# Values of four heads over a batch as a two by two block product in seven multiplications, from the third group of heads on

## The chip, the cores and the metric

The kernel runs on one core of a Trainium2 chip. The time is device microseconds of one execution, lower is better; three runs stand behind the time before. "Shares" and "busy" are of the profiled execution's span, from its first to its last instruction.

## The reference

A transformer block over x of 2 batches x 512 tokens x 512 features, all in float32. The part that the change touches is the attention's value projection:

```python
x1 = _layernorm(x)                       # 2 x 512 x 512
q, k, v = x1 @ Wq + bq, x1 @ Wk + bk, x1 @ Wv + bv    # each 512 -> 4096, 32 heads of 128
q, k = rms_norm(q, gq), rms_norm(k, gk)
attn = softmax(q k^T / sqrt(128))        # for each batch and head, 512 x 512
out = (attn @ v) @ Wo + bo               # 4096 -> 512
x = x + _layernorm(out)
```

Behind it comes a feed-forward part (a dense layer and eight gated experts of rank 16), layernorm and sum again. It isn't touched.

## The kernel before, in words

Every float32 product is made of float16 halves: an operand is scaled by a power of two and split into a high half (float16 of it) and a low half (what is left), and a product is three matmuls, high x high, high x low, low x high, added up in PSUM (`three`, lines 1234 to 1238). ScalarE makes most high halves, VectorE or GpSimd the low ones. So three matmuls stand for one, and TensorE's columns are what there is most of.

The work runs in stages. Up to some 340 us: layernorm of x, its transposed halves `xh` and `xl`, and then q and k of all 32 heads (`phase_a` on each engine), stored to DRAM; beside it GpSimd adds up squares for the norms. From there to some 1010 us: attention. Then the feed-forward part.

Attention goes by pairs of heads (`PAIRS` = 16), with the loop over two pairs at a time; `par` is 0 for an even pair, 1 for an odd one. A pair has four steps `s`, for (batch 0, head 0), (batch 0, head 1), (batch 1, head 0), (batch 1, head 1); n = 4p + s. There is no planner: each engine runs a hand-written order of its own, the function `step`, and semaphores join them. There are eight PSUM banks: four for scores, two (`YB`) for the rows of the output projection, one (`VB`) for values, one (`OB`) for the attention's output. Of a step:

- **TensorE** (`step`, line 1424): `scores` of step n, 12 matmuls of 512 columns into four banks, each bank after its low half of step n-1 is made (`low_ready`); `values`, one item of 24 matmuls of 256 columns (two tiles of 128 tokens x 256 value columns), for a pair that comes later; `rows`, 12 matmuls of the output projection, after the sums that read those banks are made (`y_added`); `attend` of step n-1, 12 matmuls.
- **VectorE** (`step`, line 2071): `maxima` of the four score banks; `add_rows`, which adds the two products of the previous step's `rows` into `y`; `inverses` (reciprocal, and `row_inv`, a scaling of five columns); `low_halves`, four; `split_v`, the low half of a value item; `scores_down` for the next step.
- **ScalarE** (`step`, line 1047): reads the output of `attend` (`o_t`); four exponentials; the high half of the next keys (`high_k`); four high halves of the probabilities, after `row_inv`; `evacuate_v`, the high half of a value item; the high half of a piece of weights.
- **GpSimd** (`step`, line 763): halves of the output (`split_o`), `scale_k`, low halves of weights (`split_wo` in steps 0 and 3, `split_wv` in steps 1 and 2: a scaling and a subtraction each), `low_k`.
- **SP's queue** (`step`, line 545): loads of q and k, of weights, and the transposes of the probabilities' halves (`pair_q` to `pair_k`).

The wait in `rows`, and the addition on VectorE that answers it:

```python
1415                        pe.wait_ge(y_added, 2 * n - 7 + k)
...
2069                    add_y(2 * n - 5 + k, 2 * ((s + 1) % 4) + k, YB + k, to).then_inc(y_added, 1)
```

The second is in `add_rows`, which step n of VectorE calls with n - 1, so both speak of the same sum.

## Time and profile before

| | before |
|---|---|
| median of 3 runs | 1071.59 us (1071.46 to 1071.72) |
| span of the profiled execution | 1069.7 us |
| median less that span (what lies around it) | 1.9 us |
| TensorE busy | 1052.9 us, 98% |
| VectorE busy | 789.6 us, 74% |
| ScalarE busy | 741.3 us, 69% |
| GpSimd busy | 681.1 us, 64% |
| granted TensorE clock, mean | 0.998 of full |
| a step of attention in the loop | 10.39 us |

The page gives the span of the profiled execution and not its whole time; the median of the runs stands for that. In the tables PE is TensorE, PEld its weight loads, DVE VectorE, ACT ScalarE, POOL GpSimd, SP SyncE. "busy" of a group is the sum of its instructions, "idle before" the time in which their engine stood still just ahead of them, with what ended it. In a timeline, "x4" is four like instructions in a row; their starts can be closer than their durations, since an operation's end overlaps the next one's start. A matmul of 512 columns shows 0.38 us, though the next begins 0.215 us later.

### The profile page before, as it was taken

What the parts mean: (1) busy time and instruction counts of PE and PEld (TensorE: products, weight loads), DVE (VectorE), ACT (ScalarE), POOL (GpSimd) and SP (SyncE); (2) the same over time, 40 slices, a digit from 0 to 9 for tenths busy, and PEclk for the clock granted to TensorE, in tenths of its full rate; (3) what the DMA queues carried; (4) which work ended last, traced back from release to release, by engine and by line L of the source; (5) the groups of instructions that cost most, each with busy time, mean ns of one, the idle gap of its engine ahead of it and who ended that gap; (6) DMA issues with size and microseconds to landing.
All of it is one profiled execution on the core that took longest, in us unless ns stands there. A gap on an engine that the chain in (4) does not pass through costs nothing.

```text
span 1069.7 us, 20038 instructions
## 1 busy us (share of the span) xinstructions
PE 1052.9 (98%) x5781; PEld 563.7 (53%) x5781; DVE 789.6 (74%) x1831; ACT 741.3 (69%) x1470; POOL 681.1 (64%) x597
## 2 busy tenths in 40 slices
PE   7999999999999999999999999999999999999997
PEld 4444444444445655555555555555555555555454
DVE  8767766666645887777777777777777777778887
ACT  4666766666656787676777767677776767777756
POOL 2667767676657476676666667666666766666713
PEclk9999999999999999999999999999999999999999
DMA  6688985656663679977676776767677676765702
GB/s 240 175 237 261 269 232 194 223 215 222 203 142 135 199 187 267 227 173 177 177 184 165 189 179 165 176 178 187 162 190 179 163 176 180 189 163 128 175 33 79
DMA packets 312072, 197.76 MB, mean 185 GB/s; under 512 B 275424, under 2 KB 279392, under 8 KB 312032
## 3 DMA queue, kind: packets, MB, share of 16 engines
q1 hardware_dynamic: 304400, 193.71, 65.5%
q10 hardware_dynamic: 7632, 3.57, 1.5%
q8 instruction: 18, 0.29, 0.1%
q14 instruction: 22, 0.18, 0.1%
HBM read 94.45 MB, written 35.68 MB: 122 GB/s over the span
## 4 chain that ended last, share of the span: by engine, by line
PE 91%; DVE 5%; ACT 2%; DMA 1%; issue 1%; SPq 0%; POOL 0%; DVEq 0%; ACTq 0%
PE ps L1236 30%; PE ps L1237 30%; PE ps L1238 30%; DMA wa_stage<-w_qk 1%; DVE pair_q L2061 1%; ACT ps L1031 0%; DVE ps L2047 0%; DVE stats L1630 0%; DMA pair_k<-pair_q 0%; ACT xh L1024 0%; ACT pair_q L1040 0%; PE ps L1348 0%; DVE y L2011 0%; DVE wa_lo L1735 0%; DVE y L2172 0%
## 5 line engine op out<-in xcount | busy, mean ns | idle before, releaser
L2047 DVE TENSOR_SCALAR_CACHE_REDUCE ps<-ps,score_down 128x512 f32<-128x512 f32 x256 | 177.5, 756 | 88.6 <-PE ps L1238 87.9
L2061 DVE SCALAR_TENSOR_TENSOR pair_q<-ps,row_inv,pair_q 128x512 f16<-128x512 f32 x256 | 174.5, 744 | 54.7 <-ACT pair_q L1040 54.6
L1031 ACT ACTIVATE ps<-ps,neg_max 128x512 f32<-128x512 f32 x256 | 168.2, 657 | 44.9 <-DVE ps L2047 44.9
L1236 PE MATMUL ps<-xh,wa_hi 128*128 128x512 f16 x512 | 194.3, 379 | 1.8 <-DVE wa_lo L1735 1.8
L1237 PE MATMUL ps<-xl,wa_hi 128*128 128x512 f16 x512 | 194.3, 379 | 0.0
L1238 PE MATMUL ps<-xh,wa_lo 128*128 128x512 f16 x512 | 194.3, 379 | 0.0
L1040 ACT ACTIVATE pair_q<-ps,row_inv 128x512 f16<-128x512 f32 x256 | 154.9, 688 | 21.5 <-DVE row_inv L2054 21.5
L758 POOL CAST oth<-o_t 128x512 f16<-128x512 f32 x62 | 37.8, 609 | 201.0 <-ACT o_t L1005 200.9
L664 POOL TENSOR_TENSOR acc<-acc,squares 128x512 f32<-128x512 f32 x120 | 151.1, 1281 | 1.7 <-ACT squares L882 1.7
L1237 PE MATMUL ps<-wv_lo,xh 128*128 128x256 f16 x512 | 139.7, 273 | 0.0
L1236 PE MATMUL ps<-wv_hi,xh 128*128 128x256 f16 x512 | 139.7, 273 | 0.0
L1238 PE MATMUL ps<-wv_hi,xl 128*128 128x256 f16 x512 | 139.7, 273 | 0.0
L655 POOL TENSOR_TENSOR qk_out<-q_s,qk_out 128x512 f16<-128x512 f32 x64 | 74.8, 1170 | 95.3 <-ACT qk_out L891 95.3
L882 ACT ACTIVATE squares<-ps,q_k_bias,qk_down 128x512 f32<-128x512 f32 x128 | 99.0, 785 | 43.0 <-PE ps L1238 28.8
L1005 ACT ACTIVATE o_t<-ps,tab 128x512 f32<-128x512 f32 x62 | 42.6, 688 | 108.0 <-PE ps L1238 108.0
L1840 DVE TENSOR_SCALAR qk_out<-ps,k_b,k_g 128x512 f32<-128x512 f32 x64 | 51.8, 809 | 84.9 <-ACT squares L882 84.9
L1236 PE MATMUL ps<-wo_hi,oth 128*128 128x512 f16 x256 | 97.2, 380 | 1.3 <-DVE otl L2038 0.6
L1236 PE MATMUL ps<-k_hi,qk_in 128*128 128x512 f16 x256 | 97.2, 380 | 0.3 <-DVE qk_out L1840 0.3
L1238 PE MATMUL ps<-k_hi,qk_in 128*128 128x512 f16 x256 | 97.2, 380 | 0.0
L1237 PE MATMUL ps<-k_lo,qk_in 128*128 128x512 f16 x256 | 97.2, 380 | 0.0
L1238 PE MATMUL ps<-wo_hi,otl 128*128 128x512 f16 x256 | 97.2, 380 | 0.0
L1237 PE MATMUL ps<-wo_lo,oth 128*128 128x512 f16 x256 | 97.1, 379 | 0.0
(236 smaller groups left out, 2220.9 us busy)
## 6 DMA issues: line engine op xcount, KB each, us to landing
q_k_scratch<-qk_out SPq DMA_DIRECT2D x64, 512.0 KB, 3.9
qk_in<-q_k_scratch SPq DMA_DIRECT2D x64, 512.0 KB, 3.4
wa_stage<-w_qk SPq DMA_DIRECT2D x32, 512.0 KB, 4.8
u_stage<-w_vo SPq DMA_DIRECT2D x32, 512.0 KB, 5.5
wv_stage<-w_vo SPq DMA_DIRECT2D x16, 512.0 KB, 4.2
wo_stage<-w_vo SPq DMA_DIRECT2D x16, 512.0 KB, 4.4
qk_tops<-qk_top_scratch ACTq DMA_DIRECT2D x27, 128.0 KB, 4.2
y<-x SPq DMA_DIRECT2D x8, 256.0 KB, 5.4
```

Source lines behind the costliest of these rows:

```text
L655: pool.tensor_tensor(pair(qk_out[:, par, b, 1, :])[:, 1, :], q_s[:, par, b * S:(b + 1) * S], pair(qk_out[:, par, b, 1, :])[:, 0, :], ALU.s ...
L664: pool.tensor_tensor(acc[:, w, cols], acc[:, w, cols], squares[:, par, w, cols], ALU.add).then_inc(acc_ready, 1)
L882: act.activation(squares[:, par, w, b * S:(b + 1) * S], ps[:, 4 * par + g, :], ACT.Square, bias=q_k_bias[:, par, w:w + 1], scale=qk_down[: ...
L1005: act.activation(o_t[:, s % 2, :], ps[:, OB, :], ACT.Identity, bias=tab[:, 4, bass.ds(h, 1)], scale=O_DOWN).then_inc(o_t_ready, 1)
L1031: act.activation(ps[:, SCORE + i, :], ps[:, SCORE + i, :], ACT.Exp, bias=neg_max[:, sl, i:i + 1], scale=-1.0, accum_out=row_sum[:, sl, i:i ...
L1040: act.activation(pair_q[:, 0, i, :], ps[:, SCORE + i, :], ACT.Identity, scale=row_inv[:, sl, i:i + 1]).then_inc(high_ready, 1)
L1236: pe.matmul(outp, lhs[0], rhs[0], start=first, stop=False)
L1237: pe.matmul(outp, lhs[0], rhs[1], start=False, stop=False)
L1238: return pe.matmul(outp, lhs[1], rhs[0], start=False, stop=last)
L1840: dve.tensor_scalar(qk_out[:, par, b, 0, :], ps[:, 4 * par + 2 * b + 1, :], k_b[:, slot:slot + 1], k_g[:, slot:slot + 1], ALU.add, ALU.mul ...
L2047: dve.tensor_scalar(ps[:, SCORE + i, :], ps[:, SCORE + i, :], score_down[:, sl, i:i + 1], None, ALU.mult, ALU.min, accum_out=neg_max[:, sl ...
L2061: dve.scalar_tensor_tensor(out=pair_q[:, 1, i, :], in0=ps[:, SCORE + i, :], scalar=row_inv[:, sl, i:i + 1], in1=pair_q[:, 0, i, :], op0=AL ...
```

## The change

The value projection of one batch is a product of 512 tokens x 512 features with 512 features x 512 columns, for four heads (two pairs). It is cut into blocks of 256: A11, A12, A21, A22 of x and B11 to B22 of the weights. Plain, that is eight block products. The new form uses seven products of sums of blocks and adds the results up (the scheme known as Winograd's form of Strassen's). It is used for 24 of the 32 heads: the first 8 heads (two groups of four) keep the old form. What changes, engine by engine:

- **Ahead of the loop**: GpSimd makes the four sums of x, each in halves, for both batches (`sums_of_x`, 32 operations, spread over eight rounds of its stage of the projections, whose loop is unrolled for it).
- **Weights**: a group's two pairs are loaded into two buffers. GpSimd makes four differences of blocks (`first_term`, `second_terms`, `fourth_term`); ScalarE seven high halves, VectorE seven low halves (`low_block`), which GpSimd made before (`split_wv`, four per group, goes).
- **Products** (`products`): a "window" of four steps (one pair) makes the values of one batch of a group: two products of 12 matmuls of 256 columns in steps 0, 1 and 3, one in step 2, in the banks `OB` and `VB`. The window of batch 0 is run in the odd pair before the group, that of batch 1 in the group's own even pair. Windows fill pairs 3 to 14.
- **Results**: ScalarE reads two of a window's products to SBUF (`v_first`, `v_fourth`), VectorE adds five up (`plus`), GpSimd two (`join`, in the next pair); ScalarE makes four high halves, GpSimd four low ones (`low_alpha` in steps 2 and 3, `low_beta` in step 1 of the next pair).
- **Items of the old form** are taken forward: steps 1.0 to 1.2 (pair 1, steps 0 to 2) make one, steps 1.3 to 2.2 two each, step 2.3 none. Steps 0 to 3 of pair 15 make no values.
- Some powers of two for the scaling change, `vh` and `vl` are twice as wide, and semaphores are shared, to no effect on the order.

The core of the diff. Lists of steps and of waits are shortened at "...":

```diff
+            def first_term(quad):
+                pool.wait_ge(wv_loaded, 16 * (quad + 2))
...
+                pool.wait_ge(second_loaded, 16 * quad)
+                pool.tensor_tensor(wt_1[:, :, :], wv_second[:, 0:2, :], wv_stage[:, 0:2, :],
+                                   ALU.subtract).then_inc(v_terms, 1)
...
+            def second_terms(quad):
+                q = quad - W_FROM
+                pool.wait_ge(v_terms, 4 * q + 1)
...
+                pool.wait_ge(wt_lo_ready, 7 * q + 1)
+                pool.tensor_tensor(wv_stage[:, 0:2, :], wv_second[:, 2:4, :], wt_1[:, :, :],
+                                   ALU.subtract).then_inc(v_terms, 1)
+                pool.tensor_tensor(wv_second[:, 0:2, :], wv_second[:, 2:4, :], wv_second[:, 0:2, :],
+                                   ALU.subtract).then_inc(v_terms, 1)
+            def fourth_term(quad):
+                pool.wait_ge(v_terms, 4 * (quad - W_FROM) + 3)
+                pool.tensor_tensor(wt_4[:, :, :], wv_stage[:, 2:4, :], wv_stage[:, 0:2, :],
+                                   ALU.subtract).then_inc(v_terms, 1)
+            def join(w):
+                pool.wait_ge(v_saved, 2 * w + 2)
...
+                pool.wait_ge(v_added, 5 * w + 5)
+                pool.tensor_tensor(v_joint, v_third[:, :, :], v_fourth[:, :, :], ALU.add).then_inc(v_joined, 1)
+                pool.tensor_tensor(v_fourth[:, :, :], v_second[:, :, :], v_fourth[:, :, :],
+                                   ALU.add).then_inc(v_joined, 1)
+            def low_beta(w, b):
+                for i, src in ((1, v_joint), (0, v_fourth[:, :, :])):
+                    pool.wait_ge(beta_high, 2 * w + 2 - i)
+                    pool.tensor_tensor(v_tiles(vl, b, i, 1), src, v_tiles(vh, b, i, 1),
+                                       ALU.subtract).then_inc(beta_ready, 1)
+            def low_alpha(w, b, i):
+                pool.wait_ge(alpha_high, 2 * w + 2 - i)
+                pool.tensor_tensor(v_tiles(vl, b, i, 0), v_sum[:, :, :], v_tiles(vh, b, i, 0),
+                                   ALU.subtract).then_inc(alpha_ready, 1)
...
+            def step(p, s, par, prepare=True, weights=True, left=None, terms=None, first=False, half=None, window=None):
                 n = 4 * p + s
                 split_o((s - 2) % 4, n - 2)
                 if prepare:
                     scale_k(p + s // 2, (s + 2) % 4)
+                if left is not None and s == 0:
+                    join(left[0])
+                if left is not None and s == 1:
+                    low_beta(*left)
+                if window is not None and s >= 2:
+                    low_alpha(*window, 3 - s)
                 if weights:
                     if s == 0:
-                        split_wo(p, par, 1, n - 2)
-                    if s == 1:
-                        split_wv(p + 1, 1 - par, 0, n - 2)
+                        split_wo(p, par, 1)
+                    if s == 3:
+                        split_wo(p + 1, 1 - par, 0)
+                if terms is not None:
+                    if s == (2 if first else 1):
+                        first_term(terms)
                     if s == 2:
-                        split_wv(p + 1, 1 - par, 2, n - 2)
+                        second_terms(terms)
                     if s == 3:
-                        split_wo(p + 1, 1 - par, 0, n - 2)
+                        fourth_term(terms)
+                if half is not None:
...
+            def values_early(w, b, s):
+                if s == 0:
+                    act.wait_ge(v_part, 7 * w + 1)
+                    act.activation(v_first[:, :, :], bank_of_values(OB), ACT.Copy, scale=V_DOWN).then_inc(v_saved, 1)
+                if s >= 2:
+                    act.wait_ge(v_added, 5 * w + 1 + s)
+                    act.activation(v_tiles(vh, b, 3 - s, 0), v_sum[:, :, :], ACT.Copy).then_inc(alpha_high, 1)
+            def values_late(w, b, s):
+                if s == 3:
+                    act.wait_ge(v_part, 7 * w + 7)
...
+                        act.wait_ge(beta_ready, 2 * w)
+                    act.activation(v_fourth[:, :, :], bank_of_values(VB), ACT.Copy, scale=V_DOWN).then_inc(v_saved, 1)
...
+            def product(left, block, b, bank):
+                for t in range(2):
+                    for k, half in enumerate(left(b, t)):
+                        ins = three(ps[:, bank, t * WIDE:(t + 1) * WIDE], half,
+                                    (wt_hi[:, block, k], wt_lo[:, block, k]), k == 0, k == 1)
+                ins.then_inc(v_part, 1)
...
+                if s != 2:
+                    pe.wait_ge(o_t_ready, n - 1)
+                if s == 0:
+                    block_ready(1)
...
+                    product(a(0, 0), B11, b, OB)
+                    block_ready(2)
...
+                        pe.wait_ge(v_saved, 2 * w)
+                    product(x_sum_of(1), T2, b, VB)
+                if s == 1:
+                    block_ready(3)
+                    product(x_sum_of(2), T3, b, OB)
+                    block_ready(4)
+                    pe.wait_ge(v_added, 5 * w + 1)
+                    product(a(1, 1), T4, b, VB)
+                if s == 2:
+                    block_ready(5)
+                    pe.wait_ge(v_added, 5 * w + 3)
+                    product(a(0, 1), B21, b, VB)
+                if s == 3:
+                    block_ready(6)
+                    product(x_sum_of(3), B22, b, OB)
+                    block_ready(7)
+                    pe.wait_ge(v_added, 5 * w + 4)
+                    product(x_sum_of(0), T1, b, VB)
...
+            def step(p, s, par, items=(), window=None, quad=None):
                 n = 4 * p + s
                 pe.wait_ge(qk_lo_ready, n + 1)
                 scores(n, s)
-                values(p, s, par, n)
+                if items:
+                    values(items[0])
+                if window is not None:
+                    products(*window[0:2], s, window[2], n)
                 rows(p, s, par, n)
-                attend(n - 1, (s - 1) % 2, (s - 1) % 4 // 2)
+                if len(items) > 1:
+                    values(items[1])
+                if window is not None:
+                    outputs_bank_read(window[0], s)
+                values_ready(s, par, quad)
...
+            def plus(to, bank, saved):
+                dve.scalar_tensor_tensor(out=to[:, :, :], in0=ps[:, bank, :].rearrange("p (t n) -> p t n", t=2),
+                                         scalar=V_DOWN, in1=saved[:, :, :], op0=ALU.mult,
+                                         op1=ALU.add).then_inc(v_added, 1)
...
+            def values_early(w, b, s):
+                if s == 1:
+                    dve.wait_ge(v_part, 7 * w + 3)
+                    plus(v_third, OB, v_second)
+                if s == 3:
+                    dve.wait_ge(v_part, 7 * w + 6)
+                    plus(v_second, OB, v_second)
+            def values_late(w, b, s):
+                if s == 0:
+                    dve.wait_ge(v_part, 7 * w + 2)
...
+                    dve.wait_ge(v_saved, 2 * w + 1)
...
+                        dve.wait_ge(v_joined, 2 * w)
+                    plus(v_second, VB, v_first)
+                if s == 1:
+                    dve.wait_ge(v_part, 7 * w + 4)
...
+                        dve.wait_ge(alpha_ready, 2 * w)
...
+                    dve.wait_ge(v_added, 5 * w + 2)
+                    plus(v_sum, VB, v_third)
+                if s == 2:
+                    dve.wait_ge(v_part, 7 * w + 5)
...
+                    dve.wait_ge(alpha_ready, 2 * w + 1)
+                    plus(v_sum, VB, v_first)
+            def low_block(quad, count, block, src):
+                dve.wait_ge(wt_hi_ready, 7 * (quad - W_FROM) + count)
+                dve.scalar_tensor_tensor(out=wt_lo[:, block], in0=src, scalar=v_up[:, :], in1=wt_hi[:, block],
+                                         op0=ALU.mult, op1=ALU.subtract).then_inc(wt_lo_ready, 1)
+            def low_early(quad, s, par):
+                if (s, par) == (2, 0):
+                    low_block(quad, 1, B11, wv_stage[:, 0:2, :])
+                if (s, par) == (0, 1):
+                    low_block(quad, 3, T3, wv_second[:, 0:2, :])
+                if (s, par) == (2, 1):
+                    low_block(quad, 6, B22, wv_second[:, 2:4, :])
+            def low_late(quad, s, par):
+                if (s, par) == (3, 0):
+                    low_block(quad, 2, T2, wv_stage[:, 0:2, :])
+                if (s, par) == (0, 1):
+                    low_block(quad, 4, T4, wt_4[:, :, :])
+                if (s, par) == (1, 1):
+                    low_block(quad, 5, B21, wv_stage[:, 2:4, :])
+                if (s, par) == (2, 1):
+                    low_block(quad, 7, T1, wt_1[:, :, :])
...
+            def step(p, s, par, items=(), rows=True, down=True, to=None, window=None, quad=None):
                 n = 4 * p + s
                 sl = s % 2
                 maxima(n, sl)
                 if rows:
                     add_rows((s - 1) % 4, n - 1, to)
+                if window is not None:
+                    values_early(*window, s)
+                if quad is not None:
+                    low_early(quad, s, par)
                 inverses(n, sl)
+                if len(items) > 1:
+                    split_v(items[0], VB)
                 for i in range(TB):
                     low_halves(n, sl, i)
-                if value:
-                    split_v(n + 2, 2 * ((s + 1) % 4), VB)
+                if items:
+                    split_v(items[-1], VB)
+                if window is not None:
+                    values_late(*window, s)
+                if quad is not None:
+                    low_late(quad, s, par)
...
+            step(1, 0, 1, items=(6,))
+            step(1, 1, 1, items=(7,))
+            step(1, 2, 1, items=(8,))
+            step(1, 3, 1, items=(9, 10))
+            step(2, 0, 0, items=(11, 12))
+            step(2, 1, 0, items=(13, 14))
+            step(2, 2, 0, items=(15, 16))
+            step(2, 3, 0)
             for s in range(4):
-                step(1, s, 1)
-            with pe.Fori(1, PAIRS // 2 - 1) as i:
+                step(3, s, 1, window=(0, 0, 0))
+            with pe.Fori(W_FROM, QUADS - 1) as i:
                 for s in range(4):
-                    step(2 * i, s, 0)
+                    step(2 * i, s, 0, window=(2 * i - 3, 1, i - 2), quad=i)
                 for s in range(4):
-                    step(2 * i + 1, s, 1)
+                    step(2 * i + 1, s, 1, window=(2 * i - 2, 0, i - 1), quad=i)
             for s in range(4):
-                step(PAIRS - 2, s, 0)
-            step(PAIRS - 1, 0, 1)
-            step(PAIRS - 1, 1, 1)
+                step(PAIRS - 2, s, 0, window=(2 * QUADS - 5, 1, QUADS - 3), quad=QUADS - 1)
+            step(PAIRS - 1, 0, 1, quad=QUADS - 1)
+            step(PAIRS - 1, 1, 1, quad=QUADS - 1)
```

## Rows read from the trace of the kernel before

**Rows 1.** The page: TensorE busy over the span, and the chain by engine.

```profile
PE 1052.9 (98%) x5781; PEld 563.7 (53%) x5781; DVE 789.6 (74%) x1831; ACT 741.3 (69%) x1470; POOL 681.1 (64%) x597
...
PE 91%; DVE 5%; ACT 2%; DMA 1%; issue 1%; SPq 0%; POOL 0%; DVEq 0%; ACTq 0%
```

**Rows 2.** Busy time by engine in one stretch of the loop, clock, DMA.

```profile
682.00:764.00 82.00, 82.00 (x476) 46.45 (x475) 62.59 (x144) 60.04 (x128) 54.43 (x48) 1.00 0.67 175
```

**Rows 3.** Timeline of one loop step: start us, duration us, engine, line, names.

```profile
702.34 0.38 PE L1236 MATMUL ps<-k_hi,qk_in 128*128 128x512 f16 x1
...
702.71 0.69 ACT L1005 ACTIVATE o_t<-ps,tab 128x512 f32<-128x512 f32 x1 [1.89 <-PE ps L1238]
...
703.19 0.76 DVE L2047 TENSOR_SCALAR_CACHE_REDUCE ps<-ps,score_down 128x512 f32<-128x512 f32 x1 [1.60 <-PE ps L1238]
...
704.93 0.27 PE L1236 MATMUL ps<-wv_hi,xh 128*128 128x256 f16 x1
...
705.37 1.28 POOL L721 TENSOR_TENSOR qk_in<-qk_in,rms_row 128x512 f32<-128x512 f32 x1
...
705.88 1.41 DVE L2005 SCALAR_TENSOR_TENSOR y<-ps,y_down,y 128x512 f32<-128x512 f32 x2
...
706.62 1.57 POOL L687 TENSOR_SCALAR wv_stage<-wv_stage,v_up 128x512 f32<-128x512 f32 x1
...
706.73 0.62 ACT L988 ACTIVATE k_hi<-qk_in 128x512 f16<-128x512 f32 x1
...
707.41 0.17 DVE L2054 TENSOR_SCALAR row_inv<-row_rec 128x5 f32<-128x5 f32 x1
...
707.55 0.38 PE L1236 MATMUL ps<-wo_hi,oth 128*128 128x512 f16 x1
...
708.52 2.73 DVE L2061 SCALAR_TENSOR_TENSOR pair_q<-ps,row_inv,pair_q 128x512 f16<-128x512 f32 x4 [0.93 <-ACT pair_q L1040]
...
711.16 0.68 DVE L1997 SCALAR_TENSOR_TENSOR vl<-ps,vh 128x512 f16<-128x512 f32 x1
...
711.75 0.22 DVE L1947 TENSOR_SCALAR score_down<-rms,exp_scale 128x5 f32<-128x5 f32 x1
...
712.73 0.38 PE L1236 MATMUL ps<-k_hi,qk_in 128*128 128x512 f16 x1
...
713.58 0.76 DVE L2047 TENSOR_SCALAR_CACHE_REDUCE ps<-ps,score_down 128x512 f32<-128x512 f32 x1 [1.60 <-PE ps L1238]
```

**Rows 4.** Timeline of the last step: two waits for a VectorE result.

```profile
1003.79 0.76 DVE L2047 TENSOR_SCALAR_CACHE_REDUCE ps<-ps,score_down 128x512 f32<-128x512 f32 x1 [0.18 <-DVE score_down L1947]
...
1008.61 2.73 DVE L2061 SCALAR_TENSOR_TENSOR pair_q<-ps,row_inv,pair_q 128x512 f16<-128x512 f32 x4
...
1009.42 0.39 PE L1236 MATMUL ps<-wo_hi,oth 128*128 128x512 f16 x1 [0.43 <-DVE pair_q L2061]
```

**Rows 5.** Groups by line and form, 560 to 1000 us: busy us, mean ns.

```profile
L2061 DVE SCALAR_TENSOR_TENSOR pair_q<-ps,row_inv,pair_q 128x512 f16<-128x512 f32 x168 | 114.5, 744 | 38.0 <-ACT pair_q L1040 38.0
...
L2005 DVE SCALAR_TENSOR_TENSOR y<-ps,y_down,y 128x512 f32<-128x512 f32 x86 | 60.5, 745 | 0.0
L721 POOL TENSOR_TENSOR qk_in<-qk_in,rms_row 128x512 f32<-128x512 f32 x42 | 53.3, 1269 | 0.0
L727 POOL TENSOR_TENSOR k_lo<-qk_in,k_hi 128x512 f16<-128x512 f32 x42 | 48.6, 1157 | 0.9 <-ACT k_hi L988 0.9
```

**Rows 6.** Timeline at 998 us: one GpSimd, one small VectorE operation.

```profile
998.11 1.16 POOL L689 TENSOR_TENSOR wb_lo<-x_first,wb_hi 128x512 f16<-128x512 f32 x1
...
998.34 0.96 DVE L2054 TENSOR_SCALAR row_inv<-row_rec 128x5 f32<-128x5 f32 x1
```

**Rows 7.** Timeline of GpSimd at 316 us, two additions of the projection stage.

```profile
316.40 2.95 POOL L664 TENSOR_TENSOR acc<-acc,squares 128x512 f32<-128x512 f32 x2
```

**Rows 8.** Timeline of VectorE at 317 us, two low halves of weights.

```profile
317.39 2.51 DVE L1735 SCALAR_TENSOR_TENSOR wa_lo<-wa_stage,qk_up,wa_hi 128x512 f16<-128x512 f32 x2
```

**Rows 9.** Waits between 60 and 380 us: total us, times, longest.

```profile
POOL qk_out L655 <- ACT qk_out L891: 84.3, 27, 10.2
```

568 lines of the change are left out of this document (397 added, 171 removed).

## The prediction, before the change was run

> **What bounds the kernel now.** I read the page first: TensorE is busy for 98% of the span and is 91% of the chain that ended last [rows 1]. A stretch of eight steps shows the same in the attention loop, at the full granted clock: 82 of 82 us on TensorE, with VectorE at 62.6, ScalarE at 60.0 and GpSimd at 54.4 [rows 2]. So columns taken off TensorE can shorten the loop, as long as no other engine comes to set its pace. Whether one does is read from the timeline of one step [rows 3]; I count from its first score matmul, T = 702.34. TensorE: scores to T+2.59, one value item (24 matmuls of 256 columns) to T+5.21, `rows` (12 matmuls) for as long as the scores, `attend` to T+10.39, where the next step begins. VectorE: four maxima from T+0.85, two additions of `y` from T+3.54, `row_inv` at T+5.07, four low halves from T+6.18, low value half at T+8.82, `score_down` at T+9.41; next maxima at T+11.24, after an idle time. Everything beside TensorE is hidden here, but VectorE is in a fixed order, and `rows` of a step waits (`y_added`) for the additions that VectorE makes in the same step, behind the maxima. The first one ends at T+3.54+0.745 = T+4.29. A matmul that waits for VectorE resumes 0.07 us after its operation's end (1008.61+0.744 to 1009.42) [rows 4], so `rows` can't start before T+4.36. It starts at T+5.21 today: cover of 0.85 us, made by the value item that the change shortens.
>
> **What is removed.** Six groups of four heads lose 24 of 192 matmuls of 256 columns each. 24 of them took 2.62 us (704.93 to 707.55) [rows 3], so 6 x 2.62 = 15.7 us come off TensorE. This is all the gain there can be.
>
> **Where the work moves.** The 58 steps from pair 1 to step 1 of pair 15 each hold one item now: 58 x 10.39 = 602.6 us. After the change:
> - Steps 0 to 2 of pair 1 are unchanged. Step 3 of pair 1 and steps 0 to 2 of pair 2 hold two items: 4 x 2.62 = +10.5 us.
> - Step 3 of pair 2 and steps 0 and 1 of pair 15 hold none. TensorE's own work would be 7.77 us, but `rows` waits until T+4.36: 4.36 + (10.39 - 5.21) = 9.54 us, so -0.85 each instead of -2.62: -2.5 us together.
> - Pairs 3 to 14 (48 steps) hold seven half items per pair: two in steps 0, 1, 3 and one in step 2. Step 2 has 10.39 - 1.31 = 9.08 us of work, its `rows` could start at T+3.90 and waits until T+4.36: 9.54 us. If nothing else ends later, a pair takes 3 x 10.39 + 9.54 = 40.71 us where it took 41.56.
>
> So even with all other engines in time the waits for the additions take 12 x 0.46 + 3 x 1.77 = 10.8 us of the 15.7.
>
> **VectorE in the loop.** From one step's maxima to the earliest possible start of the next, without any value work: 4.22 (703.19 to 707.41), 1.11 from `row_inv` to the first low half (ScalarE's high half lies between), 2.64 for the low halves, 0.22 for `score_down` and 0.17 until its result can be read (0.18 at 1003.79): 8.36 us [rows 3, 4]. The low value half that goes was 0.59 (711.16 to 711.75). What comes: ten `plus` per group, whose form is the `y` addition's (745 ns), and seven `low_block`, whose form is the low half's (744 ns) [rows 5]. At the spacing of the rows I take 0.61 and 0.68. By step: even pair 0.61, 1.22, 1.29, 1.29; odd pair 1.97, 1.90, 1.97, 0.61. Four steps are 37.9 us in an even pair and 39.9 in an odd one, against TensorE's 40.71. That would just fit.
>
> **The shared port.** It doesn't stay at that. `row_inv`, of five columns, takes 0.17 in the loop, where GpSimd is in the second half of its scaling of a weight; when it met a GpSimd TENSOR_TENSOR (998.11, 1.16 us) it took 0.96 us and ended 0.03 after it [rows 6]. Two additions of GpSimd took 2.95 us [rows 7], where twice 1.27 are 2.5, and the two low halves of weights beside them took 2.51 [rows 8], where two of the loop's four low halves (2.73 us) are 1.4: 0.55 for each. In today's loop the small operations miss GpSimd's TENSOR_TENSORs. The change puts such operations just there, after `scale_k`, which ends its turn at T+4.28 (706.62) [rows 3]; lengths are 1.27 with a float32 result and 1.16 with float16 [rows 5]:
> - Step 0: `join`, two of 1.27, T+4.28 to T+6.80. `row_inv` at T+5.07 (even) ends 0.34 late; at T+5.75 (odd, behind a `low_block`) 0.91.
> - Step 1: `low_beta`, two of 1.16, to T+6.56. `row_inv` at T+5.67 ends 0.75 late.
> - Step 2: `low_alpha` waits for ScalarE's copy (T+4.39 + 0.62 + 0.12) and for the `low_block` that started at T+4.95, so it runs T+5.70 to T+6.86: 0.97.
> - Step 3: `low_alpha` T+5.13 to T+6.29: 0.48.
>
> Together 2.5 us per even and 3.1 us per odd pair, all of it between the exponentials and the high halves, where nothing hides it. VectorE then has 40.4 us per even pair (still TensorE's 40.71) and 43.0 per odd pair, more than TensorE's. A late VectorE makes the additions late, and TensorE pays for the lateness in `rows`, with cover of 0.85 us in most steps and none in step 2.
>
> `low_block` itself has no price on this path in the trace of before. From below: none is met, nothing added (a gain is excluded: it is new work); a group takes 83.5 us, with 0.2 of the odd pair's excess absorbed. From above: I followed the four engines through eight steps by the order of the diff, each blocked operation waiting for the other's end, with `score_down` behind GpSimd's last operation and `T4` on ScalarE behind `fourth_term` (T+10.8, which makes the read of `o_t` late and through it GpSimd's next step): 40.9 + 45.2 = 86.1 us. I take three of the seven as met, 0.55 each [rows 7, 8]: 83.5 + 1.6 = 85.1 us against 83.1 today.
>
> The Trainium skill (SBUF — State Buffer, Who interferes with whom) says that a VectorE operation with two SBUF inputs contends with a GpSimd one that reads SBUF, and that the second to issue waits for the first as a whole. By that a met `low_block` costs up to GpSimd's whole 1.27; the rows here show 0.55 and the sum goes by them; with 1.27 for three a group would be 87.3.
>
> **The rest.** Sums of x: 32 GpSimd operations in the projections, four for each two heads, at 1.27 or less: under 5.1 us, where GpSimd waits 84.3/27 = 3.1 us per head [rows 9], 6.2 for two. Its results are read a head (10.4 us) later: nothing. ScalarE: 12 copies instead of 8 and 7 blocks instead of 4 per group, some 4.7 us, in its idle 1.89 us per step [rows 3]; only behind `T4` is it late, counted above. DMAs: as many bytes of weights, on the same queue; the wait on SP ahead of the load in steps 2 and 3 of odd pairs ends before the transposes' data are there. The other new waits on TensorE (`v_saved`, `v_added`, `alpha_ready`) have 1.5 us or more when VectorE is in time. The tail: the last item's columns (2.62) go from step 2 of pair 15, but the chain there is VectorE's; it loses one low value half: -0.6.
>
> **Sum.** Pair 3 has no `join` and no `low_beta`: 43.0 - 1.7 + 0.5 = 41.8. Pair 14 has no weights to make: 40.7. Five groups in between: 5 x 85.1 = 425.5. Together 508.0 against 48 x 10.39 = 498.7: +9.3. With +10.5, -2.5 and -0.6: +16.7 us. The profiled execution's span is 1069.7 and gives 1086.4; the median of the runs is 1.9 above that span and I leave this as it is: 1088 us, 1.6% slower. With a group between 83.5 and 86.1 us: 1080 to 1094.
>
> **Rivals.**
> - VectorE keeps up: the phases settle so that its small operations pass between GpSimd's. Then 12 pairs at 40.71 are -10.2, with +10.5 - 2.5 - 0.6: -2.8 us, 1068.8, faster by 0.26%. For it: the loop does this today. Against it: `low_alpha` follows ScalarE's copy, and `row_inv` always falls in it. It decides from less than about 0.2 us of blocking per odd step.
> - The full gain: `y_added` is never late, 15.7 less the tail's 2.0, 1058. It needs the additions before the maxima, which the order excludes, or steps without the cover elsewhere; I find nothing for it but my own misreading.
> - Compounding: lateness isn't made good in even pairs, which have 0.3 us to spare; they take the odd pairs' 45 us: six more times some 4 us, minus what is in the sum: about 1105.
>
> **Chances.** The forecast (1078 to 1095) 0.60; between it and the first rival (1070 to 1078) 0.13; first rival (1066 to 1070) 0.12; full gain 0.06; compounding 0.09. A measurement here can tell 0.2% (2.1 us) from no change. Faster by more: 0.08 + 0.06 + 0.01 = 0.15; within: 0.04 + 0.06 = 0.10; slower: 0.75. The range 1067 to 1096 leaves out the full gain, compounding and a bit of the first rival.
>
> **What would show it.** `row_inv` at 0.5 us or more in the mean, in place of 0.17; `low_block` with a maximum above 1 us; TensorE idle ahead of the wo matmuls of `rows`, released by the `y` addition: 0.46 in step 2 of even pairs, over 1 in odd ones, 1.77 in the steps without values; odd pairs some 3 us longer than even ones; VectorE busy for over 90% of the odd pairs. TensorE's 256-column matmuls down by 144. If the idle time ahead of `rows` is missing, the argument is wrong from its first step; if it is there in step 2 alone, the port was overrated.

## The result, and the profile after

The changed kernel took 1100.87 us (median of 4 runs, 1099.21 to 1102.26) beside 1071.65 us of the kernel before (four runs by then): ratio 1.0267, 95% interval 1.0255 to 1.0279. It is 29.2 us slower where 16.7 were predicted, above the range of 1067 to 1096. The profiled execution has a span of 1097.7 us, 28.0 more than before.

Of the page, the engines' busy time and the chain that ended last, against [rows 1]:

```profile
PE 1045.3 (95%) x5637; PEld 547.1 (50%) x5637; DVE 894.4 (81%) x1885; ACT 764.7 (70%) x1512; POOL 788.7 (72%) x677
...
PE 60%; DVE 27%; issue 5%; ACT 4%; POOL 1%; DVEq 1%; DMA 1%; SPq 0%; ACTq 0%; POOLq 0%
```

The 144 matmuls are gone (5781 to 5637), but VectorE, 5% of the chain before, is now 27% of it. The eight steps of one turn of the loop, one per line (stretch; length; busy time of each engine with its instructions; granted clock; DMA), then the even and the odd pair as wholes:

```profile
611.86:622.25 10.39, 10.39 (x62) 5.88 (x61) 9.17 (x20) 8.32 (x18) 9.60 (x9) 1.00 0.73 174
622.25:632.64 10.39, 10.39 (x62) 5.86 (x61) 8.86 (x19) 7.03 (x15) 7.86 (x8) 1.00 0.62 179
632.64:642.17 9.53, 9.25 (x49) 4.60 (x48) 8.31 (x18) 7.29 (x16) 7.43 (x7) 1.00 0.68 165
642.17:652.61 10.44, 10.44 (x62) 5.80 (x61) 9.21 (x21) 8.43 (x19) 8.01 (x8) 1.00 0.62 151
652.61:663.87 11.26, 10.56 (x62) 5.79 (x60) 10.04 (x19) 8.13 (x18) 11.04 (x10) 1.00 0.58 140
663.87:675.60 11.73, 10.61 (x62) 5.71 (x61) 10.49 (x24) 9.39 (x20) 7.28 (x7) 1.00 0.65 179
675.60:685.91 10.31, 9.25 (x50) 4.62 (x49) 9.09 (x19) 7.35 (x17) 5.63 (x5) 1.00 0.75 203
685.91:698.28 12.37, 10.56 (x61) 5.79 (x60) 11.13 (x22) 7.92 (x18) 7.68 (x7) 1.00 0.65 170
...
611.86:652.61 40.75, 40.47 (x230) 22.14 (x229) 35.54 (x75) 31.07 (x67) 32.90 (x30) 1.00 0.66 167
652.61:698.28 45.67, 40.98 (x229) 21.92 (x228) 40.76 (x80) 32.79 (x70) 31.63 (x28) 1.00 0.65 172
```

The even pair is what TensorE and the wait for the additions make it: 40.75. The odd pair has the same work on TensorE and takes 45.67. What TensorE waits for there is in its waits from 440 to 1040 us (engine, line, releaser: us, times, longest):

```profile
PE ps L1528 <- DVE y L2454: 32.7, 31, 3.1
```

And why VectorE is late is in its groups from 440 to 1000 us (line, operation, names, form, count; busy us, mean ns; idle before):

```profile
L2503 DVE TENSOR_SCALAR row_inv<-row_rec 128x5 f32<-128x5 f32 x52 | 30.8, 593 | 1.8
L2326 DVE TENSOR_SCALAR score_down<-rms,exp_scale 128x5 f32<-128x5 f32 x52 | 26.6, 512 | 0.0
L2430 DVE SCALAR_TENSOR_TENSOR wt_lo<-wv_stage,v_up,wt_hi 128x512 f16<-128x512 f32 x18 | 15.4, 856 | 0.0
L2430 DVE SCALAR_TENSOR_TENSOR wt_lo<-wv_second,v_up,wt_hi 128x512 f16<-128x512 f32 x12 | 14.3, 1193 | 0.0
L2430 DVE SCALAR_TENSOR_TENSOR wt_lo<-wt,v_up,wt_hi 128x512 f16<-128x512 f32 x12 | 10.7, 895 | 0.0
```

Two operations on five columns take 593 and 512 ns in the mean, where 0.17 and 0.22 us were the loop's [rows 3]; before, over the same stretch:

```profile
L1947 DVE TENSOR_SCALAR score_down<-rms,exp_scale 128x5 f32<-128x5 f32 x54 | 12.2, 227 | 0.0
L2054 DVE TENSOR_SCALAR row_inv<-row_rec 128x5 f32<-128x5 f32 x54 | 10.0, 186 | 1.9
```

One meeting, in step 0 of an odd pair (timeline: start, duration):

```profile
657.98 1.27 POOL L800 TENSOR_TENSOR qk_tops<-v_third,v_fourth 128x512 f32<-128x512 f32 x1
659.20 1.27 POOL L801 TENSOR_TENSOR v_fourth<-v_second,v_fourth 128x512 f32<-128x512 f32 x1
660.45 2.00 POOL L756 TENSOR_SCALAR wo_stage<-wo_stage,o_up 128x512 f32<-128x512 f32 x1
```

```profile
657.87 1.41 DVE L2454 SCALAR_TENSOR_TENSOR y<-ps,y_down,y 128x512 f32<-128x512 f32 x2
659.19 1.83 DVE L2430 SCALAR_TENSOR_TENSOR wt_lo<-wv_second,v_up,wt_hi 128x512 f16<-128x512 f32 x1
660.94 0.18 DVE L2501 RECIPROCAL row_rec<-row_sum 128x5 f32<-128x5 f32 x1
661.15 0.44 DVE L2503 TENSOR_SCALAR row_inv<-row_rec 128x5 f32<-128x5 f32 x1
```

The low block of T3 is there for the whole of the second addition of `join` and ends 0.55 us after it: 1.83 us for an operation that takes 0.74 us where it meets nothing.

### The profile page after: what moved, and what is told of

The parts are those of the page before. It is cut to its first block, busy times and chain, and to the rows that moved or that the text cites. A ratio compares the mean times of both kernels' runs of the same rounds, so it can differ in the third digit from the quotient of the medians.

```text
span 1097.7 us, 19815 instructions
## 1 busy us (share of the span) xinstructions
PE 1045.3 (95%) x5637; PEld 547.1 (50%) x5637; DVE 894.4 (81%) x1885; ACT 764.7 (70%) x1512; POOL 788.7 (72%) x677
## 4 chain that ended last, share of the span: by engine, by line
PE 60%; DVE 27%; issue 5%; ACT 4%; POOL 1%; DVEq 1%; DMA 1%; SPq 0%; ACTq 0%; POOLq 0%
PE ps L1528 20%; PE ps L1530 20%; PE ps L1529 20%; DVE ps L2496 7%; DVE pair_q L2510 5%; DVE y L2454 4%; DVE wt_lo L2430 3%; ACT pair_q L1268 2%; DVE row_inv L2503 2%; DVE score_down L2326 1%; DVE v_sum L2388 1%; DVE v_second L2388 1%; DVE stats L2009 1%; ACT y L1453 0%; DMA pair_k<-pair_q 0%
## 5 line engine op out<-in xcount | busy, mean ns | idle before, releaser
L2510 DVE SCALAR_TENSOR_TENSOR pair_q<-ps,row_inv,pair_q 128x512 f16<-128x512 f32 x256 | 174.5, 745 | 52.3 <-ACT pair_q L1268 52.3
L733 POOL TENSOR_TENSOR acc<-acc,squares 128x512 f32<-128x512 f32 x120 | 159.2, 1347 | 1.6 <-ACT squares L1079 1.6
L1528 PE MATMUL ps<-wo_hi,oth 128*128 128x512 f16 x256 | 97.8, 382 | 33.4 <-DVE y L2454 32.7
L724 POOL TENSOR_TENSOR qk_out<-q_s,qk_out 128x512 f16<-128x512 f32 x64 | 78.4, 1227 | 45.8 <-ACT qk_out L1088 45.8
L1528 PE MATMUL ps<-pair_k,vh 128*128 128x512 f16 x252 | 96.5, 383 | 3.3 <-POOL otl L939 2.6
L1046 ACT ACTIVATE wa_hi<-wa_stage,qk_up 128x512 f16<-128x512 f32 x64 | 42.8, 719 | 76.9 <-DVE qk_up L2066 76.9
L1529 PE MATMUL ps<-pair_k,vh 128*128 128x512 f16 x252 | 96.3, 382 | 0.0
L1530 PE MATMUL ps<-pair_k,vl 128*128 128x512 f16 x252 | 96.0, 381 | 0.0
```

What stands on the lines that cost most here:

```text
L724: pool.tensor_tensor(pair(qk_out[:, par, b, 1, :])[:, 1, :], q_s[:, par, b * S:(b + 1) * S], pair(qk_out[:, par, b, 1, :])[:, 0, :], ALU.s ...
L733: pool.tensor_tensor(acc[:, w, cols], acc[:, w, cols], squares[:, par, w, cols], ALU.add).then_inc(acc_ready, 1)
L1528: pe.matmul(outp, lhs[0], rhs[0], start=first, stop=False)
L1529: pe.matmul(outp, lhs[0], rhs[1], start=False, stop=False)
L1530: return pe.matmul(outp, lhs[1], rhs[0], start=False, stop=last)
L2510: dve.scalar_tensor_tensor(out=pair_q[:, 1, i, :], in0=ps[:, SCORE + i, :], scalar=row_inv[:, sl, i:i + 1], in1=pair_q[:, 0, i, :], op0=AL ...
```

## The experiments

Three theories. **Port** (the prediction's word): VectorE's chain became the limit because `row_inv`, `score_down` and the low blocks wait while GpSimd works. **Order**: it is the place of the additions of `y` behind the maxima that turns lateness into idle time of TensorE. **Volume**: VectorE simply has too many operations. A name with b_ is the kernel before with an edit, one with a_ the changed kernel with an edit; T is a step's first score matmul. Pairs below are the time from the first score matmul of a pair to that of the next, in the profiled execution of each kernel; ratios are to the kernel before on the same chip, and times of runs from different chips are best compared by them.

| kernel | us | ratio (95%) | even pair | odd pair |
|---|---|---|---|---|
| after | 1100.9 | 1.0267 (1.0255 to 1.0279) | 40.75 | 45.67 |
| b_half | 1062.8 | 0.9905 (0.9882 to 0.9928) | 40.70 | 40.70 |
| b_half_first | 1067.9 | 0.9952 (0.9936 to 0.9967) | 41.06 | 41.05 |
| b_half_first_free | 1053.4 | 0.9818 (0.9802 to 0.9835) | 40.25 | 40.25 |
| b_free | 1071.0 | 0.9991 (0.9981 to 1.0000) | 41.56 | 41.56 |
| a_first | 1101.2 | 1.0263 (1.0242 to 1.0285) | 41.81 | 43.95 |
| a_first_free | 1079.7 | 1.0072 (1.0052 to 1.0093) | 41.28 | 41.27 |
| a_free | 1078.6 | 1.0056 (1.0039 to 1.0073) | 40.71 | 41.84 |
| a_pool_short | 1094.2 | 1.0202 (1.0185 to 1.0219) | 41.08 | 44.52 |
| a_block_short | 1078.6 | 1.0064 (1.0045 to 1.0083) | 40.71 | 41.70 |
| a_mid | 1092.3 | 1.0183 (1.0168 to 1.0199) | 40.43 | 44.77 |
| a_mid_free | 1077.3 | 1.0043 (1.0030 to 1.0057) | 40.27 | 42.11 |
| a_placed | 1077.2 | 1.0034 (1.0024 to 1.0045) | 40.27 | 42.61 |
| a_placed_first | 1082.4 | 1.0091 (1.0065 to 1.0117) | 40.25 | 42.85 |
| a_placed_shared | 1092.5 | 1.0175 (1.0155 to 1.0194) | 40.44 | 45.20 |
| a_spread | 1066.4 | 0.9936 (0.9918 to 0.9954) | 40.26 | 40.83 |
| a_spread_t3 | 1074.1 | 1.0009 (0.9997 to 1.0021) | 40.26 | 41.92 |

### The wait for the additions, in the kernel before

b_half is the kernel before with half of the value item of step 2 (two of four chunks of the inner dimension; the rest of those values is left out); b_half_first also calls the additions ahead of the maxima.

```diff
-                v_item(slot, 2 * ((s + 1) % 4), VB)
+                v_item(slot, 2 * ((s + 1) % 4), VB, C // 2 if s == 2 else C)
```

```diff
-                maxima(n, sl)
                 if rows:
                     add_rows((s - 1) % 4, n - 1, to)
+                maxima(n, sl)
```

> The kernel before, with half of the matmuls of the value item left out in step 2 of each pair (12 instead of 24, so the values are wrong there); nothing else is changed. If `rows` waits for the additions of y behind the maxima, as the prediction has it, each such step takes 9.54 us and not 9.08, TensorE idles 0.46 us ahead of the wo matmuls, and the kernel is 14 x 0.85 = 11.9 us faster than before, 1060 us. If columns off TensorE count in full, it is 14 x 1.31 = 18.3 us, 1053 us.

> As b_half (half of the value item left out in step 2 of each pair), with VectorE's two additions of y moved ahead of the maxima of the same step, into the time in which it waits for scores. If the order of these two is what makes `rows` wait, the step takes 9.08 us: 18.3 us off, 1053 us. If something else ends `rows`' wait, it stays at b_half's time.

Of b_half, one step 2, and in it the first matmul of `rows` with the additions it waits for:

```profile
659.98:669.51 9.53, 9.25 (x49) 4.60 (x48) 7.71 (x18) 7.51 (x16) 6.80 (x6) 1.00 0.56 139
```

```profile
663.52 1.41 DVE L2005 SCALAR_TENSOR_TENSOR y<-ps,y_down,y 128x512 f32<-128x512 f32 x2
...
664.33 0.39 PE L1236 MATMUL ps<-wo_hi,oth 128*128 128x512 f16 x1 [0.28 <-DVE y L2005]
```

9.53 us, with `rows` at T+4.35 (664.33 less 659.98): the prediction's step on the cover of 0.85 us holds to 0.01 us, in a kernel without any other part of the change. The kernel took 1062.8 us where 1060 was expected; in the profiled execution (1064.3) the looped steps are as expected, and 3.1 us lie in step 3 of the first pair (12.38 us instead of 9.23), during which the granted clock fell to half for 3.4 us. b_half_first missed its 1053 by 15 us: the wait was gone, but `row_inv` came later in the step, into GpSimd's subtraction, and took 694 ns in the mean. So port and order were both alive, and the next kernels take away the port alone.

### The small operations without the port

"free" gives the two operations a form that also writes a minimum to a spare column; they compute the same, and each is followed by a read-out of 0.08 us:

```diff
                 dve.tensor_scalar(row_inv[:, sl, :], row_rec[:, sl, :], P_UP, None,
-                                  ALU.mult).then_inc(inv_ready, 1)
+                                  ALU.mult, ALU.min, accum_out=spare[:, sl:sl + 1]).then_inc(inv_ready, 1)
```

and `score_down` likewise. It was tried behind the reordered additions, without them, and in the kernel before.

> The changed kernel with VectorE's additions of y ahead of the maxima. Order theory: the 0.5 us in step 2 of even pairs and the 1.8 us in the steps without values go (some 8 us), and the odd pairs keep most of their length, since VectorE has as much to do: about 45 us per odd pair, 1086 to 1093 us in all. Rival, that the late additions alone make the odd pairs long: odd pairs fall to 40.3 us and the kernel to 1065 us.

> As a_first, and the two small VectorE operations (`row_inv`, `score_down`) in the form that also writes a minimum (as the maxima have), which should not need the port shared with GpSimd; 0.14 us more each. Port theory: both keep their 0.2 us beside GpSimd's operations, some 5 us per group of four heads go, odd pairs come to 40.5 to 42 us and the kernel to 1063 to 1070 us, faster than before. If VectorE's added work and not the port is what counts, it stays within 3 us of a_first.

> The changed kernel with row_inv and score_down in the form that also accumulates (a minimum into a spare column), in the order of the changed kernel. Port theory: the two small operations no longer wait for GpSimd (0.16 and 0.21 us in every step), the wait of rows for the additions stays (9.54 in step 2 of even pairs), low_block is still blocked in some places: a group of eight steps 40.8 + 41.5 = 82.3 us instead of 86.4, steps 7 to 10 of the program a few tenths less; 1100.9 - 5 x 4.1 - 1 = 1079 us. Rival, that the place of the additions behind the maxima is what costs: the group stays above 85 us, over 1093 us.

> The kernel before with half a value item in step 2 and the additions ahead of the maxima (1067.9 us in the earlier run, where 1053 was expected), now with row_inv and score_down in the accumulating form. If the blocking of row_inv by GpSimd is all that took the gain there, every step falls back to TensorE's own work, 10.39 us and 9.08 in step 2: 58 steps, 14 or 15 of them 1.31 shorter: 1053 us. Rival, that other operations (the low halves, ScalarE behind GpSimd) came late with the swap: above 1060 us.

> The kernel before with row_inv and score_down in the accumulating form. In its loop both miss GpSimd's operations and TensorE is never late, so there is nothing to gain there: 1071.5 us, ratio 0.999 to 1.001. If the form itself were faster or the small operations were blocked in places that count, the time would fall below 1069.

`row_inv` from 440 to 1000 us in b_half_first, in b_half_first_free, and in a_free:

```profile
L2054 DVE TENSOR_SCALAR row_inv<-row_rec 128x5 f32<-128x5 f32 x55 | 38.2, 694 | 1.9
```

```profile
L2055 DVE TENSOR_SCALAR_CACHE_REDUCE row_inv<-row_rec 128x5 f32<-128x5 f32 x55 | 8.8, 159 | 1.9
```

```profile
L2503 DVE TENSOR_SCALAR_CACHE_REDUCE row_inv<-row_rec 128x5 f32<-128x5 f32 x54 | 8.6, 159 | 1.9
```

159 ns in both free ones. In a_free 51 of these 54 overlap a TENSOR_TENSOR of GpSimd, and none takes more than 161 ns; in the changed kernel those that overlap one take up to 1239. The form is worth 14.5 us in the kernel before with half an item (1067.9 to 1053.4), 21.5 us in a_first (1101.2 to 1079.7) and 22.3 us in the changed kernel (1100.9 to 1078.6), and 0.1% (0.0 to 0.2) in the kernel before (b_free), where one `row_inv` of 54 was held up. b_half_first_free and a_free came as expected; a_first_free did not (1079.7 where 1063 to 1070 was expected).

The order of a_first gave nothing (1101.2 where 1086 to 1093 was expected), though TensorE's wait for `y` from 440 to 1040 us fell from 32.7 to 1.9 us. Others took its place, the longest:

```profile
PE ps L1528 <- POOL vl L812: 8.6, 6, 1.6
PE ps L1528 <- POOL otl L939: 7.4, 4, 4.0
PE ps L1528 <- DVE v_second L2388: 6.9, 6, 1.2
```

So in the order of the changed kernel some 22 of the 29.2 us go when two operations of five columns can't be held up.

The low halves (L2510), of the same operation as the low blocks but with their first input in PSUM, kept a mean of 745 ns on the page of the changed kernel, and the longest of the 256 took 754; they are never held up:

```profile
L2510 DVE SCALAR_TENSOR_TENSOR pair_q<-ps,row_inv,pair_q 128x512 f16<-128x512 f32 x256 | 174.5, 745 | 52.3 <-ACT pair_q L1268 52.3
```

### Less work on GpSimd, less on VectorE

a_pool_short leaves out all but 8 of 256 columns of `join`, `low_beta` and `low_alpha` in the loop, a_block_short the same of each low block there; the rest of those values, or of those halves of weights, isn't made (`n` is the first 8 columns of a tile; one of the four GpSimd operations is shown):

```diff
-                pool.tensor_tensor(v_tiles(vl, b, i, 0), v_sum[:, :, :], v_tiles(vh, b, i, 0),
+                pool.tensor_tensor(v_tiles(vl, b, i, 0)[:, :, n], v_sum[:, :, n], v_tiles(vh, b, i, 0)[:, :, n],
```

```diff
-                dve.scalar_tensor_tensor(out=wt_lo[:, block], in0=src, scalar=v_up[:, :], in1=wt_hi[:, block],
+                dve.scalar_tensor_tensor(out=wt_lo[:, block][:, :, n], in0=src[:, :, n], scalar=v_up[:, :], in1=wt_hi[:, block][:, :, n],
```

> The changed kernel with GpSimd's value operations (join, low_beta, low_alpha) on 8 of 256 columns of each tile from the second window on; the rest of those values is left out. VectorE has all its new work. Port theory: row_inv falls to 0.17 in all steps but those where it meets a weight operation, low_alpha no longer delays score_down; VectorE's own chain is 37.9 us per even and 39.9 us per odd pair plus blocked low_blocks, so both pairs go at the pace of the wait for the additions, 40.7 to 41.5: group 82 us, 1100.9 - 5 x 4.4 - 1 = 1078 us. Rival, that VectorE has too many operations whatever GpSimd does: group above 84.5, over 1090 us.

> The changed kernel with low_block on 8 of 256 columns of each tile in the looped groups; the rest of the low halves of the combined weights is left out there. VectorE loses 7 x 0.68 us per group and with it whatever those operations wait for GpSimd, while row_inv and score_down are as blocked as before. Port theory: 5.3 us less in VectorE's chain of the odd pair and 1.4 in the even one's; TensorE's floor of 40.71 for a pair is reached in the even pair and nearly in the odd one: group 81.8 us, 1100.9 - 5 x 4.6 = 1078 us. Rival, that the lateness comes from ScalarE and GpSimd and not from VectorE's own volume: group above 84.5, over 1091 us.

a_pool_short missed: 1094.2 where 1078 was expected, with odd pairs of 44.52. Its `row_inv` from 440 to 1000 us, and one step 2 of an odd pair:

```profile
L2509 DVE TENSOR_SCALAR row_inv<-row_rec 128x5 f32<-128x5 f32 x52 | 27.8, 534 | 1.8
```

```profile
681.16 0.59 POOL L818 TENSOR_TENSOR vl<-v_sum,vh 128x16 f16<-128x16 f32 x1 [2.06 <-ACT vh L1203]
681.72 1.15 POOL L912 TENSOR_TENSOR k_lo<-qk_in,k_hi 128x512 f16<-128x512 f32 x1
681.81 1.08 DVE L2509 TENSOR_SCALAR row_inv<-row_rec 128x5 f32<-128x5 f32 x1
```

With `low_alpha` short, `low_k` moved up by as much, and `row_inv` met that instead: 534 ns in the mean, where I had expected 0.17 us in most steps. So it isn't the added operations of GpSimd alone that block: one that was there before does it too when it stands in that place. The run tests less than it set out to, since a short operation of GpSimd still took 0.59 us. a_block_short came as expected (1078.6), with `row_inv` as blocked as ever (715 ns): VectorE's chain can be relieved at either end, so this run doesn't part port from volume; a_free does, which keeps the volume and gains the same.

### Where the rest goes, and a version that is faster than both

With the small operations free, the changed kernel was still some 6 us slower than before (ratio 1.0056). a_mid_free puts the first addition ahead of the fourth maximum only (`maxima` calls its new argument there); a_mid is the same without "free".

```diff
-                maxima(n, sl)
+                maxima(n, sl, (lambda: add_rows((s - 1) % 4, n - 1, to, (0,))) if rows else None)
                 if rows:
-                    add_rows((s - 1) % 4, n - 1, to)
+                    add_rows((s - 1) % 4, n - 1, to, (1,))
```

> The changed kernel with the accumulating row_inv and score_down, and the first addition of y ahead of the fourth maximum, the second behind it. The first addition then ends at T+3.6 instead of T+4.29, so rows can start at TensorE's own time even in step 2 (T+3.90): even pairs 10.39 x 3 + 9.08 = 40.25 instead of 40.70. The last exponential starts 0.67 us later, which costs VectorE some 0.3 us per step: odd pairs stay at 41.2 to 41.9, since VectorE sets them. Steps without values 8.9 instead of 9.6. Expected 1078.6 - 6 x 0.45 - 6 x 0.4 - 3 x 0.7 = 1071.5 us (1068 to 1075). Rival, that VectorE's later chain costs as much as the early addition gives, as with both additions first: 1079 us.

> The changed kernel with the first addition ahead of the fourth maximum and nothing else. The wait of rows goes in the even pairs' step 2 (9.08) and in the steps without values, but row_inv comes later, deeper into GpSimd's operations, and stays blocked (0.5 us or more in the mean), so that odd pairs stay at 45 to 46: expected 1100.9 - 6 x 0.45 - 2 = 1096 us, up to 1101. Rival, that the place of the additions is the cause by itself: below 1085 us.

In a_mid_free even pairs went to 40.27, TensorE's own work, and the odd ones got no shorter (42.11): 1077.3 where 1068 to 1075 was expected. a_mid took 1092.3, some 9 us less than the changed kernel, so an order can give something even with the old form; its `row_inv` fell to a mean of 361 ns while `score_down` rose to 585. With the free form the same move gave 1.3 us. a_placed adds four moves: `fourth_term` ahead of `split_wo` on GpSimd, `low_block` of T3 from ahead of `row_inv` to behind the low halves, the early sums of values behind `row_inv`, `last_factors` into step 60.

> As the kernel with the accumulating small operations and the first addition ahead of the fourth maximum (1077.3 us), and four operations moved: GpSimd's fourth term ahead of its split of the output weight, the low block of T3 from ahead of row_inv to behind the low halves of the same step, the early value sums into the idle time between row_inv and the first low half, the factors of the last part from ahead of step 60 to behind its row_inv. If these four hold the rest: the read of o_t in step 0 of odd pairs no later than 1.2 us (was 2.3) and that step 10.39, odd pairs 40.3 to 40.8 instead of 41.9 to 42.1, step 60 at most 10 us instead of 12.0: 1077.3 - 6 x 1.4 - 2 = 1067 us, faster than before by 0.4%. Rival, that VectorE has simply too much to do in odd pairs: they stay at 41.5 or more, and the time at 1073 or more.

> The same, with both additions of y ahead of the maxima instead of one ahead of the fourth. The wait for the additions has then 0.7 us more of cover and the exponentials come 0.6 us later. If VectorE's chain sets the odd pairs, this is 0.5 us per pair slower than with one addition: 1070 to 1073 us; if only the wait for the additions counts, the same as with one addition.

> The same as with the four moves, but row_inv and score_down in their old form. If it is the waiting of these two that costs most, whatever the order of the rest: row_inv at 0.4 us or more in the mean, the groups 3 us longer than in the accumulating form, 1067 + 15 = 1082 us (1078 to 1090). Rival, that the moves give the two enough room: within 3 us of the accumulating form.

The rival's numbers came, not the forecast: 1077.2, odd pairs 42.61. `o_t` in step 0 of odd pairs is read at T+0.95 instead of T+2.3, but the two low blocks that now stand together there took 1.18 and 1.64 us. a_placed_shared, 1.4% slower than a_placed by the ratios, shows the price of the old form again in another order: 15 us, as expected, on top of a kernel that was itself 10 us over its forecast. a_placed_first was 5 us slower than a_placed with the looped odd pairs only 0.24 longer. The traces place the rest, and not its reason: pair 3 takes 43.0 us instead of 40.4, and the program from step 60 on 2.1 us more, with the clock at half for 6.8 us of pair 15 where it is 3.4 in a_placed. The last two put T3 back (a_spread) or leave it (a_spread_t3), and give the low block of B21 to GpSimd, which scales and subtracts it in step 1 of odd pairs, behind `low_k`:

```diff
+                pool.tensor_scalar(wv_stage[:, 2:4, :], wv_stage[:, 2:4, :], v_up[:, :], None,
+                                   ALU.mult).then_inc(v_scaled, 1)
...
+                pool.tensor_tensor(wt_lo[:, B21], wv_stage[:, 2:4, :], wt_hi[:, B21],
+                                   ALU.subtract).then_inc(wt_lo_ready, 1)
```

> Accumulating small operations, the first addition ahead of the fourth maximum, early value sums behind row_inv, the fourth term ahead of the split of the output weight, the last factors behind step 60's row_inv, and the low block of B21 made by GpSimd in step 1 of odd pairs (1.56 + 1.16 us in its idle time there) instead of VectorE; the low block of T3 at its old place. VectorE's chain in odd pairs falls by 0.7 us or more: odd pairs 41.0 instead of 42.1, even ones 40.3: 1077.2 - 6 x 1.2 = 1070 us, 0.2% faster than before. If VectorE's load is not what is left: 1075 or more.

> The same with the low block of T3 behind the low halves, as in the run with the four moves (1077.2 us). There both low blocks of step 0 met GpSimd's operations and cost 2.8 us together; they still do: 1072 to 1075 us, slower than with T3 at its old place.

a_spread took 1066.4 us, ratio 0.9936 (0.9918 to 0.9954): faster than the kernel before by 0.6%, with the whole change in it, where 1070 was expected. What the moves would give without the change wasn't run, but for the free form (b_free, 0.1%). Its even and odd pair:

```profile
605.56:645.82 40.26, 40.26 (x230) 22.23 (x228) 33.53 (x84) 31.75 (x68) 33.18 (x30) 1.00 0.67 169
645.82:686.67 40.85, 40.62 (x229) 21.92 (x228) 36.15 (x86) 32.51 (x69) 33.51 (x29) 1.00 0.73 193
```

TensorE is busy in all but 0.23 of 81.1 us. VectorE is busy for 69.7 us of the two pairs, where it was 76.3, though only one low block of 0.74 us has left it: the rest is waiting that is no longer counted as its work. The place of T3 alone, the one difference to a_spread_t3 (1074.1, as expected), is 1.1 us per odd pair.

## Why the prediction was right or wrong

- **The cover of 0.85 us and the wait for `y_added`**: right. Steps 2 of even pairs took 9.53 us (9.54 predicted), two of the three steps without values 9.61 (9.54 predicted), shown alone by b_half.
- **Two items in one step, +10.5**: right; four steps of 13.01, 13.01, 13.01 and 13.31, 0.3 more for a blocked `row_inv` (1.24 us) and low block (1.14) in the last.
- **The shared port**: right as the cause, by five comparisons of one form against the other. Its terms were off singly, and that they are right as a sum is luck: per odd pair `row_inv` adds 1.44 us to 4 x 0.17 (3.1 predicted), `score_down` 1.82 to 4 x 0.22 (nothing in the sum), the low blocks 1.67 to 0.74 each (1.65 predicted, three at 0.55; it was 1.09, 0.37 and 0.22): 4.9 against 4.8. In an even pair `row_inv` adds 2.2 (2.5 predicted) and `score_down` 0.8 (nothing in the sum).
- **The step that failed is the sum by pairs.** I put VectorE's 40.4 us of an even pair against TensorE's 40.71 and called it even, and had an odd pair start on time. But VectorE can't work ahead: in steps 0 and 1 it waits for the scores, and what it has to spare there is lost. The first maxima of steps 2 and 3 and of the odd pair's step 0, the first of them still waiting for TensorE's scores:

```profile
633.49 0.76 DVE L2496 TENSOR_SCALAR_CACHE_REDUCE ps<-ps,score_down 128x512 f32<-128x512 f32 x1 [0.26 <-PE ps L1530]
...
643.92 0.76 DVE L2496 TENSOR_SCALAR_CACHE_REDUCE ps<-ps,score_down 128x512 f32<-128x512 f32 x1 [0.25 <-DVE score_down L2326]
...
655.18 0.76 DVE L2496 TENSOR_SCALAR_CACHE_REDUCE ps<-ps,score_down 128x512 f32<-128x512 f32 x1 [0.26 <-DVE score_down L2326]
```

From one to the next steps 2 and 3 of the even pair take 10.43 and 11.26 us, where TensorE's steps are 9.53 and 10.44. So the odd pair starts with its maxima at T+2.57 instead of T+0.85, 1.72 us late, and TensorE pays for that in its first steps: an odd pair of 45.67 where I had 44.4 (85.1 less 40.7). That is 1.3 us in each of five groups, 6.5 in all; the 48 steps grew by 15.8 us (514.5 against 498.7) where the sum said 9.3. The upper bound, followed step by step, had 86.1 per group; measured were 86.4. I took the value nearest to the sum by pairs instead.
- **Step 60**: 12.72 us instead of 9.54. Its maxima start at T+2.28: `last_factors`, a chain of small operations on VectorE ahead of it, had been hidden by the cover that the change takes away. I named every operation that moves, but not those that stay and lose their cover. In a_placed, which has it behind `row_inv` and the first addition early, the step takes 8.94. The rest of step 60 is the clock, below. Together 3.2 us; in a_block_short, where the clock doesn't fall there, the step takes 11.04.
- **The tail**: +0.7 instead of -0.6. The clock falls again in step 62, which takes 9.56 us; in a_block_short, without the fall, it takes 7.95.

In the profiled executions, in order of time, against steps of 10.39: +10.5 and +0.3 (two items), -0.8 (step 3 of pair 2), +15.8 (the 48 steps), +2.3 and -0.8 (steps 0 and 1 of pair 15), +0.7 (tail): 28.0 us, the difference of the spans. The rivals: VectorE doesn't keep up; the compounding one (1105) was nearer than the forecast, though by another way, since even pairs do make good what an odd one leaves (maxima at T+0.91 and T+0.85 in their steps 0 and 1).

The low block of T3 waited 1.09 of the 1.27 us of `join`'s second addition. The Trainium skill (SBUF — State Buffer, Who interferes with whom) has the second operation wait for the first as a whole. The trace nearly agrees: the two starts lie 0.01 us apart, so it doesn't show which was second, and the low block ended 0.55 us after the addition, less than its own 0.74. The price of 1.27 for each of three low blocks, which gave 87.3 us for a group, is not borne out: three were held up and cost 1.67 together. The same section excepts from the scalings that take the shared ports the form that also writes out its accumulator; a_free agrees, 159 ns where the other form took 593.

## What to carry to other kernels

Compare engines step by step, not by the sum over several steps: an engine that waits for its input in one step can't save that time for the next. When a change shortens the engine that sets the pace, list everything that its cover hid, also what the change doesn't touch. And a small operation that is nearly free can be so by phase alone; if a form exists that isn't held up, as the accumulating one here, it makes the time independent of what the neighbour does there.

## What the hardware showed that I had not expected

- The clock of TensorE. In step 60 of the changed kernel (columns as in the stretches above):

```profile
998.27:1005.30 7.03, 3.92 (x19) 1.67 (x18) 6.45 (x22) 4.30 (x11) 5.80 (x6) 1.00 0.72 141
1005.30:1008.70 3.40, 3.40 (x10) 1.21 (x9) 2.98 (x5) 3.40 (x7) 3.32 (x3) 0.51 0.00 0
```

After a stretch in which TensorE was busy for 3.92 of 7.03 us, the granted clock was 0.51 for 3.4 us, the lower of its two levels (1.2 of 2.4 GHz), which costs about 1.7 us; it came again from 1025.8 to 1029.2 us. a_block_short has the same stretch in its step 60, 3.94 us busy of 7.04, and its clock stays up behind it; the step takes 11.04 us:

```profile
978.64:985.68 7.04, 3.94 (x19) 1.69 (x18) 6.45 (x22) 4.32 (x11) 5.81 (x6) 1.00 0.65 140
985.68:989.10 3.42, 3.42 (x18) 1.54 (x16) 3.01 (x5) 3.42 (x7) 3.34 (x3) 1.00 0.00 0
```

What decides is open. The four runs of the changed kernel lie near 1099.4 and near 1102.2 us; the mean granted clock is 0.995 in all four, so it doesn't part them, and what does is open.
- GpSimd is held up too: its scaling of a weight that began while the low block still ran took 2.00 us (660.45), where 1.57 is the group's mean in a_free.
- An operation of five columns took up to 1.24 us (`row_inv`; `score_down` up to 1.22), where GpSimd's on 512 columns beside it take 1.16 to 1.27.
